# The last round in another order of units, with its first tiles' output and the feed-forward tiles in flight beside them

## The chip, the cores and the metric

The kernel runs on one core of one Trainium2 chip. The metric is device time in microseconds (us) of one execution, lower is better. The engines are TensorE (PE: matmuls into the PSUM banks; PEld: its weight loads), VectorE (DVE), ScalarE (ACT), GpSimd (POOL) and SyncE (SP, which issues DMAs). Each works through its own instructions in order and waits on semaphores for the others.

## The reference

One pre-norm transformer layer in float32 for 4 batches of 1024 tokens of width 128: attention with 16 heads of width 64, then a gated feed-forward layer of width 352 whose inputs and weights are rounded blockwise to FP4 values.

```python
def fp4_quant_dequant(x):                       # blocks of 16 along the last dim
    scale = jnp.maximum(jnp.max(jnp.abs(xb), axis=-1, keepdims=True) / 6.0, 1e-12)
    idx = jnp.searchsorted(_MID, jnp.abs(xb / scale))
    return (_GRID[idx] * jnp.sign(xb / scale) * scale).reshape(x.shape)
def fp4_linear(x, w):
    return jnp.einsum('bsk,nk->bsn', fp4_quant_dequant(x), fp4_quant_dequant(w))
# attention: e = exp(sim - max); attn = e / (sum(e) + 1e-10); out = (attn @ v) @ Wo.T + bo
x = x + attention(layernorm(x))
n = layernorm(x)
x = x + fp4_linear(silu(fp4_linear(n, w_gate)) * fp4_linear(n, w_up), w_down)
```

## The kernel before

**Rounds and units.** The 64 pairs of batch and head are taken two heads at a time: 32 pairs (NPAIR), one for each round. There are 34 rounds, 0 to 33; a round attends its own pair, projects keys, queries and values for the next one, and finishes the output of the one before. A round has four units k = 0 to 3, each one head with one half (512 rows) of the queries, and a unit has eight slots s = 0 to 7, one for each 128 keys. Unit k was head k // 2, half k % 2: both halves of head 0, then both of head 1. Round 33 has no units left; it holds the last unit's products with the values and what remains of pair 32.

**A slot.** TensorE makes two matmuls of scores into one of two banks (L628, L630), ScalarE takes the exponential (L781), GpSimd subtracts its rounded part (L475, "product" or "low part" in what follows), and TensorE multiplies the unit before with the values (L655, L657, L650). TensorE may run only two slots ahead of the exponentials. After each unit ScalarE copies the result (L750), VectorE makes the denominator and its reciprocal (L946, L948), and ScalarE scales (L791, in slots 3 and 4 of the unit behind the copy).

**Jobs.** All other matmuls are jobs in the table JOBS (L51): a name, a bank, and the places (unit, slot) at which TensorE, ScalarE and VectorE do their parts. `t` turns the normalised output, half 0 or 1; `o` projects it and VectorE adds it to x (L940). `x`, `g`, `u`, `h`, `d` are the feed-forward layer of two token tiles at a time: turn the input, gate, up, turn the hidden values, down. Between `u` and `h` the hidden values are quantised in ten steps (`quant`, L1088) at the places AT_H_BEGIN and AT_H (L66): nine on VectorE, and one, a scaling called the rounding step here, on ScalarE (`lift_steps`, L1139, at AT_H_LIFT). `runs` (L105) says in which rounds a job is done, `job_before`, `job_ready` and `job_ahead` (L124 to L148) which job's semaphore a wait names. Feed-forward tiles start as soon as their batch is through attention; the last two before the tail (n = 11) have `g` and `u` in round 32 and `h` and `d` in round 33.

**The tail.** The last batch's eight tiles can be normalised only when pair 32 is added. VectorE takes statistics of four tiles (`late_stats`, L1428), GpSimd the root (L1331), VectorE normalises and quantises them (`late_x`, L1440), for half 0 and then half 1. The last step of a quantisation is GpSimd's (`end`, L1320). Then come four groups of two tiles: TensorE gate and up (L1371, L1372), ScalarE the tanh, GpSimd the gate product (L1344), VectorE the product with up and the next quantisation (L1466, L1103 to L1125), TensorE the turn and down (L1379, L1386). In round 33, VectorE did the statistics of half 0 at (1, 7) and those of half 1 and `late_x(0)` at (2, 7):

```python
                            if (k, s) == (2, 7):
                                dve.wait_ge(s_x2, 2 * NPAIR)
                                ffn.late_stats(dve, x2, 1)

                                dve.wait_ge(s_pv, 4 * NPAIR)
                                ffn.late_x(dve, x2, 0)
```

Of the kernel before, what the change touches and what calls it, by code (L numbers as in the profile page):

```python
# [15 lines left out]
P = 128  # L16
# [43 lines left out]
        ("v1", X0, (3, 5), (3, 6), (3, 6))]  # L60
# [14 lines left out]
AT_X_LIFT, AT_H_LIFT = (3, 5), (0, 5)  # L75
FIRST_FFN = PAIRS + 1
# [46 lines left out]

def job_before(r, n):  # L124

    for back in range(2):
        if r - back < 0:
            return None
        for m in reversed(range(n if back == 0 else len(JOBS))):
            if JOBS[m][1] == JOBS[n][1] and runs(r - back, m):  # L130
                return m, back
    return None


def job_ready(g, r, n):

    def of(r, last=len(JOBS)):
        return sum(1 for m in range(last) if JOBS[m][1] == JOBS[n][1] and runs(r, m))
    return sum(of(a) for a in range(r)) + of(r) * (g - r) + of(r, n + 1)
# [33 lines left out]
def build(nc, x, wq, wk, wv, wo, bo, w_gate, w_up, w_down, out):  # L173
    with ExitStack() as ctx:
# [124 lines left out]
        def output_of(g, q, k):  # L299

            pq, pk = (q, k - 2) if k >= 2 else (1 - q, k + 2)
            return 4 * (g - 1) + k - 2, pq, pk // 2, (pk % 2) * IT

        def taken(m, g):
# [7 lines left out]
            if name[0] == "t":  # L312
                return s_ot, 2 * (g - 2) + c + 1
            if name[0] == "o":
                return s_x2, 2 * (g - 2) + c + 1
# [25 lines left out]
        def _(sp):  # L341
# [9 lines left out]
            def round_(g, r, q):  # L351
                prev, cur, nxt = flags(r)

                def place_max(k):

                    head, half = (k + 1) // 2 % 2, (k + 1) % 2
# [124 lines left out]
        def _(pe):  # L481
# [45 lines left out]
            def job(name, g, r, q, n):  # L527
# [27 lines left out]
                elif name[0] == "t":  # L555

                    wait(pe, s_on, 8 * (g - 1) - 2 * (1 - c))
                    for t in range(4):
                        last = pe.transpose(bank[:, t * P:(t + 1) * P], o_n[1 - q][:, 4 * c + t, :], ident[:, :])  # L559
                elif name[0] == "o":  # L560

                    wait(pe, s_ot, 2 * (g - 2) + c + 1)
                    for t in range(4):
                        last = pe.matmul(bank[:, t * P:(t + 1) * P], oT[:, (4 * c + t) * P:(4 * c + t + 1) * P],  # L564
                                         wo_s[:, bass.ds((g - 2) % PAIRS, 1), :].rearrange("p a n -> p (a n)"),
# [14 lines left out]
            def round_(g, r, q):  # L580
# [6 lines left out]
                for k in range(4):  # L587
                    head, half = k // 2, k % 2
                    unit = 4 * (g - 1) + k

                    def scores(d):

                        n = 2 * q + 1 if k < 2 else 2 * (1 - q)
                        h = n % 2
                        if k % 2 == 0 and d == 0:
                            wait(pe, s_dkh[h], 32 * (g + (1 if k else 0)))
                            wait(pe, s_dqh[h], 32 * (g + (1 if k else 0)))
# [904 lines left out]
```

## Time and profile before

| | us |
|---|---|
| median of 3 runs | 1441.13 (1439.35 to 1445.4) |
| the profiled execution, device time | 1440.82 |
| its span | 1437.8 |
| PE busy | 1341.8 (93%) |
| DVE busy | 1123.0 (78%) |
| ACT busy | 1134.4 (79%) |
| POOL busy | 1143.5 (80%) |
| exponentials, L781, 1024 of them | 775.3 |
| POOL products, L475, 1024 of them | 1080.3 |

Times in the profile count from the span's start. An instruction's row gives its start and length; "idle" is how long its engine stood before it, and the arrow names what released it. A busy share is an average over stages: the change touches only what lies between some 1352 us (unit 2 of round 32) and 1395 us, so those stages are what to read. The last unit's exponentials end at 1369.95, the last VectorE instruction begins at 1435.27.

### The profile page before, as it was taken

Reading aid. Unit: us, or ns where it says so; the run is one execution under the profiler, and the core shown is the slowest. Engines: PE = TensorE matmul, PEld = TensorE weight load, DVE = VectorE, ACT = ScalarE, POOL = GpSimd, SP = SyncE. Lnnn points to the kernel's source line nnn. Section 1 sums busy time; section 2 is a strip of 40 time slices with the busy share of each in tenths; the row PEclk is TensorE's granted clock in tenths of the full one; section 3 lists DMA queues with packets and bytes.
Section 4 is the critical chain, followed back from the end, with each engine's and each line's share of the span. In section 5 each row is a group of like instructions: output and inputs, shape, how many; then the busy total and the mean of one; then the engine's idle time right before and its main releaser. Section 6 shows DMA issues by size and latency. Waiting matters only on the chain.

```text
span 1437.8 us, 43018 instructions
## 1 busy us (share of the span) xinstructions
PE 1341.8 (93%) x17924; PEld 880.5 (61%) x17924; DVE 1123.0 (78%) x1717; ACT 1134.4 (79%) x2285; POOL 1143.5 (80%) x1135
## 2 busy tenths in 40 slices
PE   3899999999999999999999999999999999999956
PEld 2466666666666666666666666666666666666644
DVE  7777777778778878787887878888787888878677
ACT  2698887978888887888788888888888888788842
POOL 5688988878888878788887888888888888888832
PEclk8899999999999999999999999999999999999986
DMA  7111111112211111122111111211122121112000
GB/s 178 46 46 46 46 41 28 28 42 46 46 46 46 29 44 28 46 50 46 46 28 34 40 46 45 50 35 38 24 49 46 46 50 24 42 31 50 2 5 15
DMA packets 46687, 60.26 MB, mean 42 GB/s; under 512 B 8672, under 2 KB 21920, under 8 KB 46496
## 3 DMA queue, kind: packets, MB, share of 16 engines
q1 hardware_dynamic: 46336, 57.26, 17.0%
q8 instruction: 143, 2.34, 0.7%
q14 instruction: 48, 0.39, 0.1%
q10 hardware_dynamic: 160, 0.26, 0.1%
HBM read 4.80 MB, written 2.10 MB: 5 GB/s over the span
## 4 chain that ended last, share of the span: by engine, by line
PE 69%; DVE 21%; ACT 6%; issue 3%; DMA 1%; POOL 1%; SPq 0%; DVEq 0%
PE st L628 13%; PE st L630 11%; DVE negm L959 8%; PE sm L610 8%; PE ob L650 7%; PE ob L657 6%; PE ob L655 6%; ACT probs L781 3%; PE sm L548 2%; PE sm L1258 2%; PE mb L564 2%; PE sm L564 2%; DVE qv L1113 2%; PE mb L548 2%; PE sm L553 2%
## 5 line engine op out<-in xcount | busy, mean ns | idle before, releaser
L475 POOL TENSOR_TENSOR p_low<-probs 128x512 f16<-128x512 f32 x1024 | 1080.3, 1075 | 231.7 <-ACT probs L781 214.2
L781 ACT ACTIVATE probs<-st,lift,exp_scale 128x512 f32<-128x512 f32 x1024 | 775.3, 772 | 164.2 <-PE st L630 156.3
L959 DVE TENSOR_REDUCE negm<-sm 128x1 f32<-128x1024 f32 x512 | 616.2, 1214 | 204.8 <-PE sm L610 204.5
L628 PE MATMUL st<-q_hl,k_hh 128*128 128x512 f16 x1024 | 391.9, 383 | 6.8 <-ACT probs L781 6.7
L630 PE MATMUL st<-q_hm,k_l 128*128 128x512 f16 x1024 | 388.9, 380 | 0.0
L655 PEld LDWEIGHTS ob<-v,probs 128*128 128x128 bf16 x4096 | 289.7, 99 | 60.9 <-ACT o_raw L750 1.1
L655 PE MATMUL ob<-v,probs 128*128 128x65 f16 x4096 | 319.3, 193 | 0.7 <-ACT o_raw L750 0.7
L657 PE MATMUL ob<-v,probs 128*128 128x64 f16 x4096 | 319.8, 194 | 0.0
L657 PEld LDWEIGHTS ob<-v,probs 128*128 128x128 bf16 x4096 | 270.6, 97 | 59.9
L650 PEld LDWEIGHTS ob<-v,p_low 128*128 128x128 f16 x4096 | 177.1, 97 | 90.7 <-issue 1.1
L628 PEld LDWEIGHTS st<-q_hl,k_hh 128*128 128x128 f16 x1024 | 99.5, 97 | 154.3 <-issue 80.4
L650 PE MATMUL ob<-v,p_low 128*128 128x65 f16 x4096 | 188.1, 193 | 0.0
L610 PE MATMUL sm<-k_hh,q_hl 64*128 64x512 f16 x512 | 155.7, 384 | 10.7 <-DMA q_hm<-q_high 3.8
L610 PE MATMUL sm<-k_hh,q_hm 64*128 64x512 f16 x512 | 156.2, 385 | 0.0
L791 ACT ACTIVATE o_n<-o_raw,rden 128x64 f32<-128x64 f32 x512 | 147.1, 337 | 1.1 <-DVE rden L948 1.1
L630 PEld LDWEIGHTS st<-q_hm,k_l 128*128 128x128 f16 x1024 | 100.2, 98 | 26.8 <-issue 9.5
L716 ACT ACTIVATE oT<-sm 128x512 f32<-128x512 f32 x64 | 38.2, 597 | 37.4 <-PE sm L559 37.0
L946 DVE TENSOR_SCALAR den<-o_raw 128x4 f32<-128x4 f32 x128 | 51.4, 402 | 8.4 <-ACT o_raw L750 8.4
L564 PE MATMUL sm<-wo_s,oT 128*128 128x128 f32 x256 | 36.8, 287 | 20.7 <-DVE negm L959 19.3
L610 PEld LDWEIGHTS sm<-k_hh,q_hl 64*128 64x128 f16 x512 | 29.1, 94 | 34.5 <-issue 11.2
L750 ACT ACTIVATE o_raw<-ob 128x260 f32<-128x260 f32 x128 | 50.0, 390 | 0.0
L564 PEld LDWEIGHTS sm<-wo_s,oT 128*128 128x128 f32 x256 | 31.2, 192 | 22.5 <-DVE negm L959 20.9
(204 smaller groups left out, 1640.6 us busy)
## 6 DMA issues: line engine op xcount, KB each, us to landing
k_hh<-k_high SPq DMA_DIRECT2D x128, 128.0 KB, 2.4
k_l<-k_low SPq DMA_DIRECT2D x64, 128.0 KB, 2.4
q_hl<-q_high SPq DMA_DIRECT2D x64, 128.0 KB, 2.3
q_hl<-q_low SPq DMA_DIRECT2D x64, 128.0 KB, 2.4
q_hm<-q_high SPq DMA_DIRECT2D x62, 128.0 KB, 2.3
x<-x SPq DMA_DIRECT2D x4, 512.0 KB, 7.3
q_hm<-m_high SPq DMA_DIRECT2D x128, 1.0 KB
q_hm<-m_low SPq DMA_DIRECT2D x128, 1.0 KB
```

The costliest lines, as they stand in the source:

```text
L475: return pool.tensor_tensor(p_low[b][:, j, :], p, p.bitcast(BF16)[:, 1::2], ALU.subtract)
L548: last = pe.matmul(bank[:, :], of_pair(wT[w], "qk".index(name[0]), g), of_batch(xT[a], g, c * HALF, HALF), start=(w == 0 and a == 0), stop ...
L564: last = pe.matmul(bank[:, t * P:(t + 1) * P], oT[:, (4 * c + t) * P:(4 * c + t + 1) * P], wo_s[:, bass.ds((g - 2) % PAIRS, 1), :].rearran ...
L610: last = pe.matmul(sm_banks[2 * (1 - a) + h], q_rows[rows, t * P:(t + 1) * P], k_hh[n][rows, h * 512:(h + 1) * 512], start=True, stop=True)
L628: pe.matmul(st[s % 2][:, :], k_hh[n][:, s * P:(s + 1) * P], q_hl[n][:, half * HALF:(half + 1) * HALF], start=True, stop=False)
L630: pe.matmul(st[s % 2][:, :], k_l1[n][:, s * P:(s + 1) * P], q_hm[n][:, half * HALF:(half + 1) * HALF], start=False, stop=True).then_inc(s_ ...
L650: last = pe.matmul(ob[:, o:o + VC], p_low[1 - k % 2][:, j, t * P:(t + 1) * P], v_j[:, 1:1 + VC], start=False, stop=(j == JT - 1), skip_gro ...
L655: pe.matmul(ob[:, o:o + VC], p, v_j[:, 1:1 + VC], start=(t == 0 and j == 0), stop=False, skip_group_check=True)
L657: pe.matmul(ob[:, o + 1:o + VC], p, v_j[:, 1 + VC:1 + VC + DH], start=False, stop=False, skip_group_check=True)
L781: nc.scalar.activation(probs[k % 2][:, s, :], st[s % 2][:, :], ACT.Exp, bias=lift[:, 0:1], scale=exp_scale[:, head, pair:pair + 1]).then_i ...
L791: last = nc.scalar.activation(o_n[pq][:, tile + t, head * DH:(head + 1) * DH], o_raw[k % 2][:, t, 1:VC], ACT.Copy, scale=rden[:, k % 2, t: ...
L959: nc.vector.tensor_reduce(negm[k % 2][:, pair % 4:pair % 4 + 1], banks.rearrange("p a n -> p (a n)"), AX.X, ALU.max, negate=True).then_inc ...
```

## The change

In round 32 the units take half 0 of head 0, half 0 of head 1, then the two halves 1 (`head_half`). So half 0 of both heads is through after unit 1 instead of unit 2. That lets `t0` and `o0` of pair 32 stand in round 32 at unit 3, slots 5 and 6, and the statistics of half 0 at (3, 7); `late_x(0)` stands at (0, 0) of round 33, and GpSimd does the first quantisation's last step ahead of the second root. For the two tiles in flight `g1` and `u1` move from unit 3 (slots 1 and 2) to unit 2 (slots 5 and 6), their quantisation from round 33 to unit 3 of round 32 (AT_H_LAST), and `h0`, `h1`, `d` to slots 2, 3 and 5 of round 33's first unit, between the last unit's products. The jobs are the same in number and size. `job_before` and `job_ready` now sort by place instead of by position in the table. The gate product on VectorE also waits on `s_hm`, in all rounds.

```diff
-        ("v1", X0, (3, 5), (3, 6), (3, 6))]
+        ("v1", X0, (3, 5), (3, 6), (3, 6)),
+        ("g1", X0, (2, 5), (2, 6), (2, 6)), ("u1", X1, (2, 6), None, (2, 7)),
+        ("t0", X1, (3, 5), (3, 6), None), ("o0", X0, (3, 6), None, (3, 7)),
+        ("h0", MB, (0, 2), (0, 3), None), ("h1", X1, (0, 3), (0, 4), None), ("d", X0, (0, 5), None, (0, 6))]
+LAST = len(JOBS) - 7
+AT_H_LAST, AT_H_LAST_LIFT = ((3, 0), (3, 0), (3, 1), (3, 3), (3, 4), (3, 5)), (3, 2)
...
+def whose(r, n):
+    return r if n >= LAST else r - 1
...
+    if n >= LAST:
+        return r == (NPAIR + 1 if name in "hd" else NPAIR)
+    if (JOBS[n][0] in ("g1", "u1") and r == NPAIR) or (JOBS[n][0] in ("t0", "o0", "h0", "h1", "d") and r == NPAIR + 1):
+        return False
...
+def head_half(r, k):
+    return (k % 2, k // 2) if r == NPAIR else (k // 2, k % 2)
...
-                    head, half = k // 2, k % 2
+                    head, half = head_half(g, k)
...
+                        if r == NPAIR and (k, s) == (3, 7):
+                            dve.wait_ge(s_x2, 2 * NPAIR - 1)
+                            ffn.late_stats(dve, x2, 0)
                         if r == NPAIR + 1:
-                            if (k, s) == (1, 7):
-                                dve.wait_ge(s_x2, 2 * NPAIR - 1)
-                                ffn.late_stats(dve, x2, 0)
+                            if (k, s) == (0, 0):
+                                dve.wait_ge(s_pv, 4 * NPAIR - 1)
+                                ffn.late_x(dve, x2, 0)
                             if (k, s) == (2, 7):
                                 dve.wait_ge(s_x2, 2 * NPAIR)
                                 ffn.late_stats(dve, x2, 1)
-                                dve.wait_ge(s_pv, 4 * NPAIR)
-                                ffn.late_x(dve, x2, 0)
...
-        if n is not None and here == AT_H_LIFT:
+        if n is not None and r <= NPAIR and here == AT_H_LIFT:
+            self.lift_steps(act, 2 * FF, self.steps(n, True))
+        n = ffn_two(r, 1)
+        if n is not None and r == NPAIR and here == AT_H_LAST_LIFT:
             self.lift_steps(act, 2 * FF, self.steps(n, True))
...
-            for part, place in enumerate(AT_H_BEGIN):
+            for part, place in enumerate(AT_H_LAST if r == NPAIR else AT_H_BEGIN):
...
             dve.wait_ge(self.s_th, 2 * n + t + 1)
+            wait(dve, self.s_hm, 2 * n + t)
...
         root(0)
+        self.end(pool, 0)
         root(1)
-        self.end(pool, 0)
         self.end(pool, 1)
```

**VectorE around unit 3 of round 32.** `den` and `rden` are a unit's denominator and reciprocal, `wgu` and `hidden` the gate and up products of the tiles in flight, `q_small`, `qv`, `qw` the scratch of their quantisation. Before:

```order
L946 TENSOR_SCALAR den<-o_raw1 128x4 [waits o_taken]
L948 RECIPROCAL rden<-den 128x4 [waits sums_made]
L1289 SCALAR_TENSOR_TENSOR wgu<-xn,sm 128x352 [waits tanh_made,mb_ready1]
L1293 SCALAR_TENSOR_TENSOR hidden<-wgu,sm 128x352 [waits gate_taken,mb_ready2]
L1103 TENSOR_REDUCE q_small<-hidden 128x44 [waits hidden_made]
L1105 TENSOR_SCALAR q_small<-q_small 128x44 [waits quant_step]
L946 TENSOR_SCALAR den<-o_raw0 128x4 [waits o_taken]
L948 RECIPROCAL rden<-den 128x4 [waits sums_made]
L1109 TENSOR_SCALAR q_small<-q_small 128x44 [waits quant_step]
L1111 RECIPROCAL q_small<-q_small 128x44 [waits quant_step]
L1113 TENSOR_TENSOR qv<-hidden,q_small 128x704 [waits quant_step]
L1118 TENSOR_SCALAR qw<-qv 128x704 [waits quant_step]
```

And now:

```order
L1320 SCALAR_TENSOR_TENSOR wgu<-xn,sm 128x352 [waits hidden_made,tanh_made,mb_ready1]
L1324 SCALAR_TENSOR_TENSOR hidden<-wgu,sm 128x352 [waits gate_taken,mb_ready2]
L973 TENSOR_SCALAR den<-o_raw1 128x4 [waits o_taken]
L975 RECIPROCAL rden<-den 128x4 [waits sums_made]
L1130 TENSOR_REDUCE q_small<-hidden 128x44 [waits hidden_made]
L1132 TENSOR_SCALAR q_small<-q_small 128x44 [waits quant_step]
L1136 TENSOR_SCALAR q_small<-q_small 128x44 [waits quant_step]
L1138 RECIPROCAL q_small<-q_small 128x44 [waits quant_step]
L1140 TENSOR_TENSOR qv<-hidden,q_small 128x704 [waits quant_step]
L1145 TENSOR_SCALAR qw<-qv 128x704 [waits quant_step]
```

Gate and up stand ahead of unit 1's reciprocal instead of behind it, and the quantisation up to the mask (`qw<-qv`) follows it in one piece, where the reciprocals of units 2 and 3 stood around it.

**ScalarE at the start of unit 3 of round 32.** `o_raw1` is the copy of unit 1's result, `probs1` the exponentials, `xn<-sm` the tanh of g1, `qw<-qw` the rounding step. Before:

```order
L750 ACTIVATE o_raw1<-ob 128x260 [waits pv_done]
L781 ACTIVATE probs1<-st,lift,exp_scale 128x512 [waits pv_done,scores_t_ready]
L781 ACTIVATE probs1<-st,lift,exp_scale 128x512 [waits scores_t_ready]
L1278 ACTIVATE xn<-sm 128x352 [waits mb_ready1]
L781 ACTIVATE probs1<-st,lift,exp_scale 128x512 [waits scores_t_ready] x2
L791 ACTIVATE o_n1<-o_raw1,rden 128x64 [waits norm_step]
L791 ACTIVATE o_n1<-o_raw1,rden 128x64
```

And now:

```order
L776 ACTIVATE o_raw1<-ob 128x260 [waits pv_done]
L807 ACTIVATE probs1<-st,lift,exp_scale 128x512 [waits pv_done,scores_t_ready]
L807 ACTIVATE probs1<-st,lift,exp_scale 128x512 [waits scores_t_ready]
L1170 ACTIVATE qw<-qw 128x704 [waits quant_step]
L807 ACTIVATE probs1<-st,lift,exp_scale 128x512 [waits scores_t_ready] x2
```

The tanh left this place, and the rounding step stands here, behind two exponentials and ahead of six.

**VectorE in round 33.** `x2<-x2,sm 128x512` and `x2<-x2,mb 128x512` are the additions of o0 and o1, the one of 128x256 that of d, `p_low0<-x2` the normalisation of four tiles. Before, from the last unit's reciprocal to the first normalisation:

```order
L946 TENSOR_SCALAR den<-o_raw1 128x4 [waits o_taken]
L948 RECIPROCAL rden<-den 128x4 [waits sums_made]
...
L940 TENSOR_TENSOR x2<-x2,mb 128x512 [waits x2_added,mb_ready0]
L1297 TENSOR_TENSOR x2<-x2,sm 128x256 [waits mb_ready1]
L1433 BN_STATS stats<-x2 128x6 [waits x2_added]
...
L1445 TENSOR_SCALAR p_low0<-x2,mv,rstd 128x128 [waits ln2_root_step,pv_done]
L1445 TENSOR_SCALAR p_low0<-x2,mv,rstd 128x128 x3
L1103 TENSOR_REDUCE wd<-p_low0 128x32 [waits ln2_done]
```

And now, from the first normalisation through the last unit's reciprocal to the second statistics:

```order
L1476 TENSOR_SCALAR p_low0<-x2,mv,rstd 128x128 [waits ln2_root_step,pv_done]
L1476 TENSOR_SCALAR p_low0<-x2,mv,rstd 128x128 x3
...
L1152 TENSOR_TENSOR probs0<-probs0 128x512 [waits quant_step]
L1328 TENSOR_TENSOR x2<-x2,sm 128x256 [waits mb_ready1]
L973 TENSOR_SCALAR den<-o_raw1 128x4 [waits o_taken]
L975 RECIPROCAL rden<-den 128x4 [waits sums_made]
L967 TENSOR_TENSOR x2<-x2,mb 128x512 [waits x2_added,mb_ready0]
L1464 BN_STATS stats<-x2 128x6 [waits x2_added]
L1464 BN_STATS stats<-x2 128x6 x3
L1468 BN_AGGR mv<-stats 128x2 [waits ln2_stats_step]
```

The last unit's denominator and reciprocal stood ahead of both statistics and both normalisations; now they stand behind the first normalisation and its quantisation.

## Rows read from the trace of the kernel before

**Rows 1.** Busy time: length, then PE, PEld, DVE, ACT, POOL (with instructions), clock, DMA.

```profile
1361.60:1370.20 8.60, 7.73 (x115) 5.17 (x114) 3.36 (x6) 7.51 (x15) 8.29 (x9) 1.00 0.01 2
1370.20:1382.60 12.40, 8.78 (x138) 7.63 (x138) 9.95 (x29) 5.29 (x17) 2.60 (x4) 1.00 0.02 4
```

**Rows 2.** Chain of waits, 1388 to 1398 us; start, length, engine, tile, line.

```profile
1391.43 1.54 PE st L1371 x2
...
1397.25 0.94 POOL probs L1344
```

**Rows 3.** Timeline of ScalarE from unit 3 on; start, length, instruction, count, idle time before.

```profile
1361.42 0.38 ACT L750 ACTIVATE o_raw<-ob 128x260 f32<-128x260 f32 x1
1361.69 1.45 ACT L781 ACTIVATE probs<-st,lift,exp_scale 128x512 f32<-128x512 f32 x2
...
1363.82 0.78 ACT L781 ACTIVATE probs<-st,lift,exp_scale 128x512 f32<-128x512 f32 x1
...
1367.70 2.25 ACT L781 ACTIVATE probs<-st,lift,exp_scale 128x512 f32<-128x512 f32 x3
...
1373.61 0.79 ACT L1143 ACTIVATE qw<-qw 128x704 f32<-128x704 f32 x1 [1.69 <-DVE qw L1118]
```

**Rows 4.** Timeline of VectorE: reciprocal, six steps of the hidden quantisation, one without GpSimd.

```profile
1362.22 0.18 DVE L948 RECIPROCAL rden<-den 128x4 f32<-128x4 f32 x1
...
1365.53 0.89 DVE L1103 TENSOR_REDUCE q_small<-hidden 128x44 f32<-128x704 f32 x1
1366.45 0.90 DVE L1105 TENSOR_SCALAR q_small<-q_small 128x44 f32<-128x44 f32 x1
...
1371.66 0.43 DVE L1111 RECIPROCAL q_small<-q_small 128x44 f32<-128x44 f32 x1
1372.12 0.89 DVE L1113 TENSOR_TENSOR qv<-hidden,q_small 128x704 f32<-128x704 f32 x1
1373.05 0.53 DVE L1118 TENSOR_SCALAR qw<-qv 128x704 uint32<-128x704 uint32 x1
...
1399.69 0.18 DVE L1105 TENSOR_SCALAR wd<-wd 128x44 f32<-128x44 f32 x1
```

**Rows 5.** Timeline of VectorE from the last reciprocal to the second quantisation's end.

```profile
1375.44 0.18 DVE L948 RECIPROCAL rden<-den 128x4 f32<-128x4 f32 x1
...
1379.81 0.69 DVE L940 TENSOR_TENSOR x<-x,mb 128x512 f32<-128x512 f32 x1 [0.58 <-PE mb L564]
...
1382.68 1.08 DVE L1445 TENSOR_SCALAR p_low<-x,mv,rstd 128x128 f32<-128x128 f32 x4
...
1388.32 1.85 DVE L1445 TENSOR_SCALAR p_low<-x,mv,rstd 128x128 f32<-128x128 f32 x4
...
1394.12 0.69 DVE L1125 TENSOR_TENSOR probs<-probs 128x512 f32<-128x512 f32 x1
```

**Rows 6.** Timeline of TensorE: projection, turns, output projection, down projection, a slow turn.

```profile
1362.51 0.84 PE L1258 MATMUL sm<-wguT,xn 128*128 128x352 f32 x2
...
1376.86 0.63 PE L559 MATMUL sm<-ident,o_n 128*128 128x128 f32 x4 [0.42 <-ACT o_n L791]
...
1378.62 1.16 PE L564 MATMUL mb<-wo_s,oT 128*128 128x128 f32 x8
1379.61 1.50 PE L1269 MATMUL sm<-wdT,hiddenT 128*128 128x128 f32 x12
1389.63 1.11 PE L1362 MATMUL sm<-ident,p_low 128*128 128x128 f32 x4 [8.52 <-POOL p_low L1325]
```

**Rows 7.** Timeline of GpSimd: the last twelve products and the first root.

```profile
1358.98 12.61 POOL L475 TENSOR_TENSOR p_low<-probs 128x512 f16<-128x512 f32 x12 [0.86 <-ACT probs L781]
...
1379.60 1.01 POOL L1338 TENSOR_TENSOR rstd<-var_eps,minus_half 128x4 f32<-128x4 f32 x1
```

**Rows 8.** Stretches of one us on TensorE: length, busy time, granted clock, DMA.

```profile
1384.00:1385.00 1.00, 0.00 (x0) 1.00 0.00 0
1385.00:1386.00 1.00, 0.00 (x0) 0.50 0.00 0
```

More of the change, by code:

```diff
@@ L121, in runs, with jobs_of, job_ready @@
     return cur if JOBS[n][ON_PE][0] < 3 else nxt
+def jobs_of(r, bank):
+    return sorted((m for m in range(len(JOBS)) if JOBS[m][1] == bank and runs(r, m)), key=lambda m: (JOBS[m][ON_PE], m))
 def job_before(r, n):
[L126 to L139, printed above, removed]
+    here = jobs_of(r, JOBS[n][1])
+    at = here.index(n)
+    if at:
+        return here[at - 1], 0
+    earlier = jobs_of(r - 1, JOBS[n][1]) if r else []
+    return (earlier[-1], 1) if earlier else None
+def job_ready(r, n):
+    here = jobs_of(r, JOBS[n][1])
+    return sum(len(jobs_of(a, JOBS[n][1])) for a in range(r)) + here.index(n) + 1
+def head_half(r, k):
+    return (k % 2, k // 2) if r == NPAIR else (k // 2, k % 2)
 def has_max(r, k):
@@ L299, in output_of @@
         def output_of(g, q, k):
-            pq, pk = (q, k - 2) if k >= 2 else (1 - q, k + 2)
-            return 4 * (g - 1) + k - 2, pq, pk // 2, (pk % 2) * IT
+            pq, r, pk = (q, g, k - 2) if k >= 2 else (1 - q, g - 1, k + 2)
+            head, half = head_half(r, pk)
+            return 4 * (g - 1) + k - 2, pq, head, half * IT
         def taken(m, g):
@@ L555, in job @@
                 elif name[0] == "t":
-                    wait(pe, s_on, 8 * (g - 1) - 2 * (1 - c))
+                    pair, own = whose(g, n), whose(g, n) == g
+                    wait(pe, s_on, 8 * pair - (4 if pair == NPAIR else 2) * (1 - c))
                     for t in range(4):
-                        last = pe.transpose(bank[:, t * P:(t + 1) * P], o_n[1 - q][:, 4 * c + t, :], ident[:, :])
+                        last = pe.transpose(bank[:, t * P:(t + 1) * P], o_n[q if own else 1 - q][:, 4 * c + t, :], ident[:, :])
                 elif name[0] == "o":
-                    wait(pe, s_ot, 2 * (g - 2) + c + 1)
+                    pair = whose(g, n)
+                    wait(pe, s_ot, 2 * (pair - 1) + c + 1)
                     for t in range(4):
                         last = pe.matmul(bank[:, t * P:(t + 1) * P], oT[:, (4 * c + t) * P:(4 * c + t + 1) * P],
-                                         wo_s[:, bass.ds((g - 2) % PAIRS, 1), :].rearrange("p a n -> p (a n)"),
+                                         wo_s[:, bass.ds((pair - 1) % PAIRS, 1), :].rearrange("p a n -> p (a n)"),
                                          start=True, stop=True)
@@ L587, in round_ @@
                 for k in range(4):
-                    head, half = k // 2, k % 2
+                    head, half = head_half(g, k)
                     unit = 4 * (g - 1) + k
                     def scores(d):
[L593 to L597, printed above, removed]
+                        of = g if k < 2 else g + 1
+                        h, half = head_half(of, (k + 2) % 4)
+                        n = 2 * (q if k < 2 else 1 - q) + h
+                        if half == 0 and d == 0:
+                            wait(pe, s_dkh[h], 32 * of)
+                            wait(pe, s_dqh[h], 32 * of)
                         earlier = maxima_ahead(r, k, 4 * d - 1)
@@ L699, in take @@
                 cols = slice(c * HALF, (c + 1) * HALF)
-                ready = job_ready(g, r, m)
+                ready = job_ready(r, m)
                 if name[0] == "q":
@@ L1205, in beside_vector @@
         n = ffn_two(r, 2)
-        if n is not None:
+        if n is not None and r <= NPAIR:
             for part, place in enumerate(AT_H):
```

19 lines of the change are left out of this document (10 added, 9 removed).

## The prediction

> **What bounds the kernel now.** I read the stages first. In the last unit of the last round TensorE is busy 7.73 of 8.60 us, ScalarE 7.51 and GpSimd 8.29, while VectorE works only 3.36; in the stretch behind it VectorE works 9.95 of 12.40 [rows 1]. So the units are paced by three engines together, and behind them the end hangs on VectorE. Second, the chain of waits: the last step of the first quantisation is followed by gate and up on TensorE, a pair in 1.54 us, and later by GpSimd's second gate product, which begins at 1397.25 [rows 2]. Beside it runs the second quantisation, done at 1394.81 [rows 5]; everything later on VectorE is a fixed series behind these two. I call that time L. The question is what the change does to L, and whether what it gains before L is lost again earlier.
>
> **The two projections moved into unit 2 (g1, u1).** Each pair of matmuls stands with 0.84 us [rows 6]. They leave unit 3 and enter unit 2, so TensorE's sum over the two units doesn't change; but unit 2 ends later. Bounds 0 (all in waits) and 1.7 us (twice 0.84); I take 1.0, since some of it falls into waits that TensorE has there. The copy of unit 1's result, which opens unit 3 on ScalarE, moves from 1361.42 [rows 3] to 1362.4.
>
> **The quantisation moved into unit 3, and the wait that it brings.** Its rounding step on ScalarE (qw<-qw) stood in round 33, where nothing urgent was queued behind it. Now it stands third in unit 3, ahead of six exponentials. It waits for six VectorE instructions, which come behind the denominator and its reciprocal of unit 1; before, that reciprocal ended 0.98 us after the copy began (1361.42 to 1362.40) [rows 3, 4], so 1363.4 now. Then reduce 0.89, two steps on the block scales at 0.90 or 0.18, reciprocal 0.43, product 0.89, mask 0.53 [rows 4], and 0.15 of gaps: 4.7 us with the large figure twice, 3.25 with the small one. The large one was measured with GpSimd at work, the small one with GpSimd idle; GpSimd has its product of unit 3's second exponential until about 1365.7 and then nothing, so I take 4.1. The mask is ready at 1367.5 (1366.7 to 1368.1). With 0.79 for the rounding step [rows 3] the third exponential starts at E = 1368.3. Without the wait it could start when two exponentials behind the copy are done: 1362.4 + 0.27 + 1.45 = 1364.1. So ScalarE loses 4.2 us, 3.4 of it waiting, and all that is queued behind: six exponentials, and through them TensorE's scores and GpSimd's products.
>
> The Trainium skill (SBUF — State Buffer, section "SBUF: two separate sides") says that VectorE and GpSimd hold a shared port pair as an exclusive lock for a whole instruction. That speaks against this place, since it makes small VectorE steps wait out a GpSimd product; the trace agrees with its 0.90 beside 0.18. By the rule the wait would be at the long end while GpSimd runs and at the short end afterwards, which is the same middle.
>
> **t0 and o0 inside unit 3.** From the third exponential on, unit 3 took 1369.95 - 1363.82 = 6.1 us [rows 3]. Now ScalarE also copies the turned tile (0.6), TensorE turns it (0.63) and projects it (1.16) [rows 6], each waiting for the other. By steps: three exponentials and two pairs of scalings bring the sixth exponential to E + 3.0; the turn starts at E + 3.2 when the last scaling is done, the copy is ready at E + 4.5, the projection and the last scores are done at E + 6.1, the last exponential at E + 6.9. That is 0.8 more than before; bounds 0 and 2.4 (0.6 + 0.63 + 1.16 all exposed). Unit 3 ends at 1375.2 where it ended at 1369.95: **+5.2 us**, of which the wait is 3.4.
>
> **What is gained: the first half of the late tiles.** The sums for it now need only o0. Behind the last exponential GpSimd has one product (12.61 for twelve, so 1.05) and the root (1.01 [rows 7], some 1.35 with the small step ahead of it and the gaps): the root is ready at E + 9.4 = 1377.7. The first normalisation and quantisation therefore starts at 1377.7 instead of 1382.68, 5.0 us earlier though the unit ends 5.2 later. It takes 5.7 (from 1382.68 to the start of the next part at 1388.32 [rows 5]) and ends at 1383.4.
>
> **What that costs the second half.** The last unit's products start 0.3 behind its last exponential, 1375.5, take 3.0, now with two sets of transposes (0.4 each) and the down projection (1.35) between them, 5.1 in all; the copy of the result is done at 1380.9. Its reciprocal is queued on VectorE behind the first quantisation and the addition of d: 1383.4 + 0.4 + 0.4 = 1384.2. Before it was done at 1375.62 [rows 5]. From there the path is what it was: reciprocal to addition of o1 4.2 us (1375.62 to 1379.81), then 0.69 for the addition, 1.2 of statistics and 1.3 of root on an idle GpSimd, 5.7 of normalising and quantising (before 6.5, because its first part took 1.85 and not 1.08 [rows 5]). Sum: 1384.2 + 4.2 + 0.7 + 1.2 + 1.4 + 5.7 = 1397.4, so L moves by **+2.6**. Gate and up of the first tiles are then long done, so the second gate product follows the first directly, 0.4 less. And the turn and projection of the last output come after 4.5 us without matmuls: TensorE's last matmul ended at 1381.1 [rows 6], the granted clock was 1.00 (2.4 GHz) at 1384 and 0.50 (1.2 GHz) at 1385 [rows 8]; at half speed a turn of four tiles takes 1.11 and not 0.63 [rows 6], and the projection by the same ratio 2.0 and not 1.16, so +1.4 (bounds 0 and 1.4; I take 1.4, as a pause of 3.9 was enough there).
>
> The new wait of the gate product on hidden_made costs nothing: it stands between instructions of the same engine that are long done; bounds 0 and 24 times some 0.05, 1.2. The two swapped DMA destinations on SP are as long as before, and their data is ready a unit earlier than needed.
>
> **Sum.** +2.6 - 0.4 + 1.4 = +3.6. The profiled execution took 1440.82 for a span of 1437.8, 0.3 under the median of the runs, 1441.13. So 1444.4. What a measurement of this kernel can tell from no change is some 0.5%, 7.2 us.
>
> **Rivals.** (a) *The first half hides wholly.* The rounding step doesn't hold ScalarE, because unit 3 was slowed elsewhere anyway or VectorE's small steps run at 0.18: then the last exponential ends 3.4 earlier, and with the clock kept up L moves by +2.6 - 3.4 = -0.8, with the gate's -0.4 that is -1.2: 1439.6. For it: VectorE has 5.2 free us in unit 3 [rows 1]. Against: it is latency, not load, and the six instructions follow each other. A gain of 7 us isn't there: from the last reciprocal to L lie 13 us in series, and the last products can't end earlier than before.
>
> (b) *The wait cools TensorE.* During the 3.4 us in which ScalarE waits, TensorE runs out of work after its third group of products, since scores need free score banks. If the clock falls to 1.2 GHz there, the ten groups left in unit 3 run at half speed. TensorE's work in them is 4.6 us at full speed, about 3.2 of it would then be exposed: 1447.6, and up to 1450 if unit 3's last products are also slow. This is the case on the slower side; it decides from the point where the pause is as long as those before which the clock fell in this trace. For it: the wait is nearly as long as the pause of 3.9 us behind 1381.1, at whose end the clock fell [rows 6, 8]. Against: it held up to then, and my wait may be shorter still. The Trainium skill (TensorE: Matmul & The Clock Gate, Part 1) has the low clock as the resting state that activity lifts; by it this case would come to the same 1447.6.
>
> (c) *The order isn't what decides.* L stays with GpSimd and the gates, and both effects vanish: 1441.
>
> **Chances.** Forecast 0.50, (a) 0.20, (b) 0.22, (c) 0.08. The forecast's own range is 1442 to 1447; with (a) below and (b) above the range is 1437.5 to 1450. Faster by over 0.5% (below 1433.9) would need (a) and a luckier clock in the tail: 0.05. Slower by over 0.5% (above 1448.3): the far part of (b), 0.15. Within: 0.80.
>
> **What would show it.** In the changed profile ScalarE's qw<-qw in unit 3 should be preceded by 3 to 4 us of idle time released by VectorE's mask, GpSimd should idle as long, and the last exponential should end near 1375. VectorE's first late normalisation should start near 1378, the last output's reciprocal directly behind the addition of d, and VectorE should idle some 4 us before the addition of o1. I am wrong if the rounding step finds its input ready, if the last exponential ends before 1372, or if the second quantisation ends before 1394.

## The result and the profile after

The changed kernel took 1445.11 us (1443.44 to 1446.82, 20 runs), the kernel before 1439.88 us (1437.14 to 1445.4, 20 runs): ratio 1.0034, 95% interval 1.0027 to 1.0041, or 4.9 us (3.9 to 5.9) longer. It is a small loss.

The profiled execution after has a span of 1443.7 us against 1437.8. The two rows below, the copy on ScalarE that opens unit 2 of round 32, before (L750) and after (L776), show that it is 1.45 us later after, ahead of every instruction that the change moves. The shift was there early: ScalarE's copy of `m_high` begins at 33.12 before and 34.61 after. So the new wait of the gate product, which stands in all rounds, cost nothing that shows.

```profile
1352.21 0.40 ACT L750 ACTIVATE o_raw<-ob 128x260 f32<-128x260 f32 x1
```

```profile
1353.66 0.39 ACT L776 ACTIVATE o_raw<-ob 128x260 f32<-128x260 f32 x1
```

Over the profiles of all kernels below this offset lies between -0.02 and +2.03 us, the same kernel run twice differed by 0.75 and 1.56, and the time outside the span was 3.02 us before and 1.9 after, which nearly cancels it. So from here on times in a unit are counted from this copy, written +x. The last VectorE instruction starts at +83.06 before and +87.55 after: **4.5 us** later, which is what the two profiles give for the change.

ScalarE after, from the copy that opens unit 3 (columns as in [rows 3]):

```profile
1363.86 0.38 ACT L776 ACTIVATE o_raw<-ob 128x260 f32<-128x260 f32 x1
1364.12 1.45 ACT L807 ACTIVATE probs<-st,lift,exp_scale 128x512 f32<-128x512 f32 x2
1369.32 0.79 ACT L1170 ACTIVATE qw<-qw 128x704 f32<-128x704 f32 x1 [3.74 <-DVE qw L1145]
1370.01 1.43 ACT L807 ACTIVATE probs<-st,lift,exp_scale 128x512 f32<-128x512 f32 x2
...
1377.85 0.78 ACT L807 ACTIVATE probs<-st,lift,exp_scale 128x512 f32<-128x512 f32 x1 [1.25 <-PE st L656]
```

Unit 3 opens at +10.20 (before +9.21). The rounding step waits 3.74 us for VectorE's mask and holds six exponentials; the last of them ends at +24.97, where it ended at +17.74 [rows 3]. That last one also waited 1.25 for scores from TensorE; most of this wait isn't the clock's, since it is 1.07 in fill below, where the clock stays up: the projection of o0 stands ahead of those scores. TensorE's clock did fall in the pause. Its last matmul ahead of it began at 1366.79; length, busy time and granted clock of three stretches of one us:

```profile
1368.00:1369.00 1.00, 0.00 (x0) 1.00 0.00 0
1369.00:1370.00 1.00, 0.00 (x0) 0.83 0.00 0
1370.00:1371.00 1.00, 0.17 (x1) 0.50 0.00 0
```

The next matmul, at 1370.83, found 1.2 GHz, and so did the rest of unit 3 up to 1376. VectorE after, the steps in front of the wait (answering to [rows 4]) and the end of unit 3 into the second late normalisation ([rows 5]):

```profile
1365.23 0.85 DVE L1130 TENSOR_REDUCE q_small<-hidden 128x44 f32<-128x704 f32 x1
1366.12 1.00 DVE L1132 TENSOR_SCALAR q_small<-q_small 128x44 f32<-128x44 f32 x1
1367.15 0.18 DVE L1136 TENSOR_SCALAR q_small<-q_small 128x44 f32<-128x44 f32 x1
1367.37 0.43 DVE L1138 RECIPROCAL q_small<-q_small 128x44 f32<-128x44 f32 x1
1367.83 0.89 DVE L1140 TENSOR_TENSOR qv<-hidden,q_small 128x704 f32<-128x704 f32 x1
1368.76 0.53 DVE L1145 TENSOR_SCALAR qw<-qv 128x704 uint32<-128x704 uint32 x1
...
1381.10 1.11 DVE L1476 TENSOR_SCALAR p_low<-x,mv,rstd 128x128 f32<-128x128 f32 x4 [1.12 <-POOL rstd L1369]
...
1386.78 0.41 DVE L1328 TENSOR_TENSOR x<-x,sm 128x256 f32<-128x256 f32 x1
1387.11 0.91 DVE L973 TENSOR_SCALAR den<-o_raw 128x4 f32<-128x4 f32 x1
1388.05 0.18 DVE L975 RECIPROCAL rden<-den 128x4 f32<-128x4 f32 x1
1393.42 0.69 DVE L967 TENSOR_TENSOR x<-x,mb 128x512 f32<-128x512 f32 x1 [5.19 <-PE mb L589]
...
1396.84 1.11 DVE L1476 TENSOR_SCALAR p_low<-x,mv,rstd 128x128 f32<-128x128 f32 x4 [1.41 <-POOL rstd L1369]
```

The last unit's result was copied at 1384.25; its reciprocal came only behind the first quantisation and the addition of d. TensorE stood meanwhile, and its turn and projection ran at half clock:

```profile
1389.47 1.09 PE L583 MATMUL sm<-ident,o_n 128*128 128x128 f32 x4 [5.26 <-ACT o_n L817]
1391.34 2.05 PE L589 MATMUL mb<-wo_s,oT 128*128 128x128 f32 x8 [0.78 <-ACT oT L742]
```

They took 0.63 and 1.16 before [rows 6]. GpSimd's step that ends the second quantisation:

```profile
1402.67 1.06 POOL L1356 TENSOR_TENSOR p_low<-probs,wd 128x512 f32<-128x512 f32 x1 [5.87 <-DVE probs L1152]
```

That is +49.01, before +42.68: 6.3 us later. From there to the last VectorE instruction the program is the same, but it took 38.54 us in place of 40.38, so 1.8 us came back in the tail.

### The profile page after: what moved, and what is told of

It is laid out like the page before. It is cut to its first block, busy times and chain, and to the rows that moved or that the text cites. A ratio compares the mean times of both kernels' runs of the same rounds, so it can differ in the third digit from the quotient of the medians.

```text
span 1443.7 us, 43018 instructions
## 1 busy us (share of the span) xinstructions
PE 1349.1 (93%) x17924; PEld 884.4 (61%) x17924; DVE 1124.8 (78%) x1717; ACT 1134.5 (79%) x2285; POOL 1145.7 (79%) x1135
## 4 chain that ended last, share of the span: by engine, by line
PE 69%; DVE 21%; ACT 6%; issue 3%; POOL 1%; DMA 1%; SPq 0%; DVEq 0%
PE st L654 13%; PE st L656 11%; DVE negm L986 8%; PE sm L636 8%; PE ob L676 7%; PE ob L683 6%; PE ob L681 6%; ACT probs L807 3%; PE sm L571 2%; PE sm L1288 2%; PE mb L589 2%; PE sm L589 2%; DVE qv L1140 2%; PE mb L571 2%; PE sm L576 2%
## 5 line engine op out<-in xcount | busy, mean ns | idle before, releaser
L776 ACT ACTIVATE o_raw<-ob 128x260 f32<-128x260 f32 x128 | 50.0, 391 | 2.0 <-PE ob L676 1.8
L583 PE MATMUL sm<-ident,o_n 128*128 128x128 f32 x256 | 40.6, 282 | 5.7 <-ACT o_n L817 5.7
```

## The experiments

The theory ahead of the runs: the wait of ScalarE and the cold clock behind it cost some 5 us, the late last reciprocal some 3 more, and the unit order gains part of it back. The rivals are named in each expectation; where one speaks of GpSimd's first late product, it means `late_x(0)`, which runs on VectorE. The kernels with the last reciprocal ahead (rec_first, both, dve_both, order_only, spread and their repeats) have one edit more than their cuts below show: ahead of the tail's matmuls TensorE waits for the addition of d (`pe.wait_ge(ffn.s_fin, TWOS)`). In rec_first the tail's first turn still follows the matmul before it directly (1390.56), and in spread it waited 0.98 us for that addition. Three milestones of each profile, counted from the copy that opens unit 2: end of the last exponential; start of GpSimd's end of the second late quantisation; start of the last VectorE instruction. The last column is the distance from before that the ratio gives, with its interval.

| kernel | last exp. | second end | last DVE | runs: us against before |
|---|---|---|---|---|
| before | 17.74 | 42.68 | 83.06 | |
| changed | 24.97 | 49.01 | 87.55 | +4.9 (3.9 to 5.9) |
| lift_late | 23.29 | 47.46 | 87.61 | +3.9 (2.3 to 5.6) |
| fill | 23.34 | 47.50 | 87.29 | +4.2 (2.6 to 5.9) |
| rec_first | 24.83 | 45.81 | 84.26 | +1.3 (0.0 to 2.4) |
| both | 23.28 | 43.85 | 83.99 | +0.6 (-0.7 to 1.9) |
| flight_only | 23.35 | 47.83 | 87.91 | +6.0 (4.2 to 7.9) |
| dve_lift | 19.19 | 47.89 | 87.66 | +6.3 (4.3 to 8.2) |
| dve_both | 19.19 | 44.42 | 84.20 | +2.3 (1.0 to 3.5) |
| dve_thin | 19.20 | 43.14 | 83.29 | one run |
| order_only | 19.52 | 41.68 | 80.65 | -4.3 (-6.1 to -2.6) |
| order_again | 19.52 | 41.67 | 80.62 | -3.0 (-4.2 to -1.7) |
| spread | 19.51 | 38.62 | 77.61 | -4.0 (-5.5 to -2.4) |
| spread_again | 19.51 | 38.62 | 77.79 | -5.2 (-7.2 to -3.3) |

**lift_late: the rounding step three slots later.**

```diff
-AT_H_LAST, AT_H_LAST_LIFT = ((3, 0), (3, 0), (3, 1), (3, 3), (3, 4), (3, 5)), (3, 2)
+AT_H_LAST, AT_H_LAST_LIFT = ((3, 0), (3, 0), (3, 1), (3, 5), (3, 6), (3, 6)), (3, 5)
```

> Only the rounding step of the hidden quantisation and the three steps behind it stand later in unit 3 (slots 5 and 6 in place of 2 to 5). The wait theory: ScalarE's 3.74 us of idle time ahead of qw<-qw shrinks to under 0.7, TensorE has no long pause in unit 3 and keeps the full clock, so the last exponential ends 4 to 5.5 us earlier than in the changed kernel and the whole kernel is 3.5 to 6 us faster than it, 0 to 1.5 us slower than the kernel before. The rival, that the two added jobs t0 and o0 and not the wait make unit 3 long: less than 1 us of change against the changed kernel.

1444.53 us, ratio 1.0027 (1.0016 to 1.0039): about 1 us gained at most, not 3.5 to 6, and none at the last VectorE instruction (87.61 against 87.55). The wait was still 2.20 us, because VectorE's same six steps had grown. Its timeline:

```profile
1364.00 0.85 DVE L1130 TENSOR_REDUCE q_small<-hidden 128x44 f32<-128x704 f32 x1
1364.89 1.00 DVE L1132 TENSOR_SCALAR q_small<-q_small 128x44 f32<-128x44 f32 x1
1365.92 0.96 DVE L1136 TENSOR_SCALAR q_small<-q_small 128x44 f32<-128x44 f32 x1
1366.91 0.43 DVE L1138 RECIPROCAL q_small<-q_small 128x44 f32<-128x44 f32 x1
1367.38 1.21 DVE L1140 TENSOR_TENSOR qv<-hidden,q_small 128x704 f32<-128x704 f32 x1
1368.62 1.25 DVE L1145 TENSOR_SCALAR qw<-qv 128x704 uint32<-128x704 uint32 x1
```

The six take 5.70 us against 3.88 in the changed kernel, where GpSimd had run dry beside them. The ScalarE wait had starved GpSimd, and that had made VectorE fast: part of the cost hid the other part. Nor did TensorE keep the full clock. The copy of o0's turned tile now stood on ScalarE behind the waiting step, TensorE waited for it, and the projection ran at 0.50 of the clock; the last exponential then waited 2.41 us for its scores:

```profile
1371.99 2.05 PE L589 MATMUL sm<-wo_s,oT 128*128 128x128 f32 x8 [2.84 <-ACT oT L742]
```

**fill: fourteen extra score matmuls into a free bank while ScalarE waits** (their result is not used).

```diff
+                        if r == NPAIR and (k, s) == (3, 3):
+                            for _ in range(14):
+                                pe.matmul(sm_banks[0][:, :], k_hh[2 * q + head][:, 0:P],
+                                          q_hl[2 * q + head][:, 0:HALF], start=True, stop=True)
```

> The changed kernel with 14 extra matmuls of 512 columns (some 3 us at full clock) into a score bank that is free in that stage, behind TensorE's last work before its pause in unit 3; their result is read by nobody. ScalarE's wait stays at 3.7 us. If the clock is a cost of its own there: the granted clock stays at 1.00 through unit 3, the last exponential ends 1.5 to 2.5 us earlier than in the changed kernel, and the kernel is 1 to 2.5 us faster. If the slow clock is hidden behind ScalarE: no change within 0.5 us, or slower where the extra work delays the scores.

1444.66 us, ratio 1.0029 (1.0018 to 1.0041). This isolates the clock: the wait is untouched, the clock stays at 2.4 GHz through unit 3.

```profile
1368.24 0.79 ACT L1174 ACTIVATE qw<-qw 128x704 f32<-128x704 f32 x1 [3.74 <-DVE qw L1149]
...
1375.14 0.78 ACT L811 ACTIVATE probs<-st,lift,exp_scale 128x512 f32<-128x512 f32 x1 [1.07 <-PE st L656]
```

```profile
1363.00:1378.00 15.00, 12.81 (x185) 8.90 (x186) 11.51 (x22) 8.45 (x17) 11.14 (x11) 1.00 0.00 1
```

(Columns of the second as in [rows 1]; the clock is the 1.00 behind the counts.) The last exponential ends 1.63 us earlier. That is what the cold clock cost in unit 3. The end gains only 0.3 in the profile, since the tail took 39.79 us in place of 38.54; by the times it is 0.7, within the intervals.

**rec_first: the last unit's denominator and reciprocal inside the first late quantisation, behind its mask.**

```diff
-                        if s == 0 and (prev if k < 2 else cur):
+                        if s == 0 and (prev if k < 2 else cur) and (r, k) != (NPAIR + 1, 1):
...
-                                ffn.late_x(dve, x2, 0)
+                                ffn.late_x(dve, x2, 0, lambda: reciprocals(g, q, 1))
```

> Only the last unit's denominator and reciprocal on VectorE stand inside the first late quantisation (behind its mask) in place of behind it. If the queue behind that quantisation holds up the output projection o1: the reciprocal ends 2.5 to 3 us earlier, and o1's addition with it; TensorE's pause ahead of the last turn shrinks from 5.2 to some 2.4 us, so the clock may hold, 1.4 more. The kernel is 2.5 to 4.5 us faster than the changed one. Rival, that the second quantisation is held by something else (the root on GpSimd, or the first quantisation's own length): under 1 us.

1441.78 us, ratio 1.0009 (1.0000 to 1.0017): 3.6 us of the 4.9 gone, from one reciprocal's place. VectorE:

```profile
1385.30 0.16 DVE L974 TENSOR_SCALAR den<-o_raw 128x4 f32<-128x4 f32 x1
1385.50 0.18 DVE L976 RECIPROCAL rden<-den 128x4 f32<-128x4 f32 x1
...
1390.80 0.69 DVE L968 TENSOR_TENSOR x<-x,mb 128x512 f32<-128x512 f32 x1 [3.03 <-PE mb L589]
```

The last copy began at 1384.69 here and the reciprocal ended 0.99 us later; in the changed kernel it ended 3.98 us later. The second end comes 3.20 earlier. The part of the forecast on the clock didn't come: TensorE still stood 2.26 us ahead of the last turn, and turn and projection took 1.02 and 2.05.

**both: lift_late and rec_first together.**

> Both edits together. If the two costs are separate they add up: 6 to 10 us faster than the changed kernel, 2 to 5 us faster than the kernel before (ratio 0.9965 to 0.9985 to before). Rival, that one cost takes the other's place: no better than the better of the two alone.

1441.64 us, ratio 1.0004 (0.9995 to 1.0013). The gain is 4.3, not 6 to 10, as lift_late had already fallen short.

**flight_only: the tiles in flight as in the change; units, t0, o0 and the late tiles as before.**

```diff
-    return (k % 2, k // 2) if r == NPAIR else (k // 2, k % 2)
+    return k // 2, k % 2
...
-        ("t0", X1, (3, 5), (3, 6), None), ("o0", X0, (3, 6), None, (3, 7)),
```

> Only the in-flight tiles' part of the change: g1, u1, the last h tiles and d of the first half early, with the whole quantisation chain and its rounding step on ScalarE in unit 3 of the last round; units, score turns, late statistics and GpSimd's order as before. If the waiting rounding step is what costs (my theory: 3.7 us of ScalarE, a cold TensorE behind it, and about 1 us at unit 2), then this alone pays for it and gains only the gate: 3 to 5 us slower than before. The rival, that the costs come from the unit order and the late last reciprocal: within 1 us of before.

1444.52 us, ratio 1.0042 (1.0029 to 1.0055): this half of the change carries the whole loss, and somewhat more than the 3 to 5 us expected. Its rounding step waits the same 3.74 us for the mask.

**dve_lift: the rounding step on VectorE, so that ScalarE waits for nothing of the chain.**

```diff
+                    if part == 3:
+                        w = self.small[4][:, 0:2 * FF]
+                        dve.wait_ge(self.s_q, self.steps(n, True) + 6)
+                        nc.vector.tensor_scalar(w, w, MAGIC_HALF, None, ALU.mult).then_inc(self.s_q, 1)
```

> The changed kernel with the rounding step done on VectorE right behind the chain that makes it, so that ScalarE never waits for VectorE in unit 3 and the exponentials run through. Theory (the wait and the clock that fell in it are the cost): the last exponential ends 5 to 6 us earlier against the start of unit 3's copy, TensorE stays at the full clock through unit 3, and the kernel takes 4 to 6 us less than the changed one, so about 1440. Rival (VectorE's own queue sets the end, since GpSimd's products wait for the last reciprocal anyway): at most 2 us less.

1445.6 us, ratio 1.0044 (1.0030 to 1.0057). The local forecast held: last exponential 5.8 us earlier. The kernel gained nothing, which contradicts my theory and fits the number of its rival. Ten steps of the chain now stand on VectorE; some of them, the addition of o0 that follows, and GpSimd's products beside them:

```profile
1366.04 0.99 DVE L1132 TENSOR_SCALAR q_small<-q_small 128x44 f32<-128x44 f32 x1
...
1369.77 1.25 DVE L1145 TENSOR_SCALAR qw<-qv 128x704 uint32<-128x704 uint32 x1
1371.05 1.25 DVE L1234 TENSOR_SCALAR qw<-qw 128x704 f32<-128x704 f32 x1
1372.33 1.61 DVE L1155 SCALAR_TENSOR_TENSOR qv<-qw,qv 128x704 f32<-128x704 f32 x1
...
1375.62 0.89 DVE L1162 TENSOR_TENSOR hidden<-qv,q_small 128x704 f32<-128x704 f32 x1
1376.43 0.68 DVE L967 TENSOR_TENSOR x<-x,sm 128x512 f32<-128x512 f32 x1
```

```profile
1363.95 10.89 POOL L498 TENSOR_TENSOR p_low<-probs 128x512 f16<-128x512 f32 x9 [0.31 <-ACT probs L807]
```

From 1365.14 to 1376.51 the chain took 11.4 us and held the addition of o0, the statistics and the root behind it: the exponentials had finished at 1372.77, the reciprocal of unit 3 came at 1378.5. The queue had moved from ScalarE to VectorE. TensorE stood in it too, since the turn of the hidden values now stands between the last unit's products:

```profile
1376.66 0.87 PE L1295 MATMUL mb<-ident,hidden 128*128 128x128 f32 x3 [2.41 <-DVE hidden L1162]
```

So the second end came 1.1 us earlier (+47.89) for the 5.8 of the exponentials, and the tail took that back.

**dve_thin: dve_lift with GpSimd's eight products of unit 3 at 32 elements in place of 512** (the rest of the low part of that unit is left out).

```diff
-                            low_part(k % 2, s).then_inc(s_lp, 1)
+                            low_part(k % 2, s, 32 if (r, k) == (NPAIR, 3) else HALF).then_inc(s_lp, 1)
```

> dve_lift, in which GpSimd's eight products of unit 3 of the last round are 32 elements wide in place of 512 (the rest of that part of the output is left out). If VectorE's steps of the quantisation chain are long because GpSimd's products run beside them (theory), the nine steps behind the reciprocal take 7 to 8 us in place of the 11.2 of dve_lift, with the two-input steps at 0.9 us in place of 1.6. Rival (they are long from the queue of semaphores or from ScalarE and TensorE beside them): they stay within 10% of 11.2.

The same rows:

```profile
1364.65 0.19 DVE L1132 TENSOR_SCALAR q_small<-q_small 128x44 f32<-128x44 f32 x1
...
1366.48 0.53 DVE L1145 TENSOR_SCALAR qw<-qv 128x704 uint32<-128x704 uint32 x1
1367.04 0.53 DVE L1234 TENSOR_SCALAR qw<-qw 128x704 f32<-128x704 f32 x1
1367.60 0.89 DVE L1155 SCALAR_TENSOR_TENSOR qv<-qw,qv 128x704 f32<-128x704 f32 x1
...
1369.45 0.89 DVE L1162 TENSOR_TENSOR hidden<-qv,q_small 128x704 f32<-128x704 f32 x1
```

The ten steps (I had written nine) took 6.6 us in place of 11.4, even less than the 7 to 8 expected. One run took 1440.4 us; in its profile the last VectorE instruction starts 4.4 us earlier than in dve_lift. The second end came 4.75 us earlier, just what the chain had become shorter. So the chain is slow because GpSimd works beside it, and that is what swallowed dve_lift's gain. It also shows the end of this road, in one profile: without the wait and without that slowness the changed order only comes back to before (83.29 against 83.06), as the last reciprocal is still late.

**dve_both: dve_lift and rec_first.**

> The rounding step on VectorE as in dve_lift, and the last unit's reciprocal taken inside GpSimd's first late product, behind its mask and ahead of the rest of it. If the two costs are independent they add up: 7 to 9 us less than the changed kernel, 3 to 4 below before (1436 to 1438). If both act on the same chain (GpSimd's second product), the sum is no better than rec_first alone by more than 2 us: about 1440.

1441.45 us, ratio 1.0016 (1.0007 to 1.0024). The rival's number, not the sum. The three kernels with the reciprocal ahead stand at 84.26 (rec_first), 83.99 (both) and 84.20: the wait's removal brings nothing that shows beside it either, and the reciprocal's place brings its 3.5 us again (87.66 to 84.20).

**order_only: units, t0, o0 and the first half's statistics as in the change; the tiles in flight after the units as before; `late_x(0)` behind the last reciprocal.**

```diff
-        ("g1", X0, (2, 5), (2, 6), (2, 6)), ("u1", X1, (2, 6), None, (2, 7)),
...
-        ("h0", MB, (0, 2), (0, 3), None), ("h1", X1, (0, 3), (0, 4), None), ("d", X0, (0, 5), None, (0, 6))]
...
-                            if (k, s) == (0, 0):
+                            if (k, s) == (1, 4):
                                 dve.wait_ge(s_pv, 4 * NPAIR - 1)
                                 ffn.late_x(dve, x2, 0)
```

> Only the unit order of the last round, with the two score turns and the first half's late statistics early and the first late product between; the feed-forward tiles in flight stay where before has them, after the units. By the theory that the quantisation chain in unit 3 is the whole cost and the order the whole gain: 2 to 3 us faster than before, and spread (1435.1) is 1 to 2 us below it. Rival: the order gains nothing by itself, within 1 us of before.

1437.08 us, ratio 0.9970 (0.9958 to 0.9982): the other half of the change is a gain. In it the first late normalisation begins at +26.6, directly behind the chain's last step, and not at +30.5 as before:

```profile
1378.48 0.89 DVE L1161 TENSOR_TENSOR hidden<-qv,q_small 128x704 f32<-128x704 f32 x1
1379.29 1.11 DVE L1472 TENSOR_SCALAR p_low<-x,mv,rstd 128x128 f32<-128x128 f32 x4
```

**spread: order_only with the chain cut in two, its first six steps in unit 3, the rounding step behind unit 3's last exponential, the last reciprocal directly ahead of `late_x(0)`, and d's addition at (3, 0).**

```diff
+        ("d", X0, (2, 5), None, (3, 0))]
...
+AT_H_LAST = ((3, 3), (3, 4), (3, 5), (0, 0), (0, 0), (0, 0))
...
+        if n is not None and here == (AT_H_LIFT if r <= NPAIR else (0, 0)):
...
+            for part, place in enumerate(AT_H_LAST[:3] if r == NPAIR else AT_H_BEGIN):
+            for part, place in enumerate(AT_H if r <= NPAIR else AT_H_LAST[3:]):
```

> The unit order and early score turns of the change, the quantisation chain cut in two (its first half in unit 3 where ScalarE does not wait for it, the rounding step on ScalarE only after unit 3's last exponential), and the last reciprocal ahead of GpSimd's first product. Theory: nothing waits in unit 3, unit order gives GpSimd's products earlier: 4 to 5 us faster than before. Rival (order is not what decides, the tail takes back what is gained): within 1 us of before.

1435.08 us, ratio 0.9972 (0.9962 to 0.9983). Nothing in unit 3 waits for the chain any more; g1 and u1 are back in unit 3, and the last exponential ends at +19.51, as in order_only (+19.52), which has two of the six steps there:

```profile
1371.97 0.38 ACT L776 ACTIVATE o_raw<-ob 128x260 f32<-128x260 f32 x1
1372.24 0.79 ACT L1170 ACTIVATE qw<-qw 128x704 f32<-128x704 f32 x1
```

```profile
1376.18 0.18 DVE L975 RECIPROCAL rden<-den 128x4 f32<-128x4 f32 x1
1376.27 1.11 DVE L1473 TENSOR_SCALAR p_low<-x,mv,rstd 128x128 f32<-128x128 f32 x4
...
1385.34 1.11 DVE L1473 TENSOR_SCALAR p_low<-x,mv,rstd 128x128 f32<-128x128 f32 x4 [1.10 <-POOL rstd L1366]
```

The rounding step finds its input ready, the last reciprocal precedes the first late normalisation, and the second one starts at +32.8 where the changed kernel had it at +43.2.

**order_again and spread_again: the same two kernels on one chip**, since they had stood against different runs of before.

> The same kernel as order_only, on one chip with spread, since the two stood against different runs of before. In the profiles the last VectorE instruction came 80.65 us behind the copy that opens unit 2 here and 77.61 us in spread. If cutting the quantisation chain in two is worth what the profiles show, this kernel is 2 to 3 us slower than spread. If the tail takes that back, as the ratios 0.9970 and 0.9972 suggest, the two agree within 1 us.

> As spread: 2 to 3 us faster than order_again by the profiles, within 1 us of it by the ratios; 3 to 5 us faster than before in either case.

1438.49 and 1436.26 us, ratios 0.9979 (0.9971 to 0.9988) and 0.9964 (0.9950 to 0.9977): 2.2 us apart in the medians. The intervals of the two ratios still touch, but the runs can be compared directly: of the 55 pairs of a run of order_again (11) and one of spread_again (5), spread is the faster in 53, and the profiles say the same (2.8 to 3.0 us at the last VectorE instruction). So the cut of the chain gains some 2 us, and both kernels beat the one before.

## Why the prediction held, and where its sum was off

The forecast was 1444.4, the median 1445.11. That they lie 0.7 apart is partly luck: the forecast was 3.6 us above a profiled execution of 1440.82, and the kernel before had a median of 1439.88 in the comparison. The effect itself is +3.6 against +4.9 by the ratio and +4.5 by the profiles. Its terms by the profiles:

- **Unit 2 later by 1.0 for g1 and u1:** measured 0.99 (unit 3 opens at +10.20 in place of +9.21). Right, though it was a choice between 0 and 1.7; in order_only and spread, which leave them in unit 3, it opens at +9.20 and +9.19.
- **The wait in unit 3, 3.4 us:** measured 3.74. Right in kind, place and releaser. The six steps took 4.06 us with gaps, and I had taken 4.1; the reciprocal ahead of them ended 1.45 us behind the copy's start and not 0.98, since the denominator took 0.83 beside GpSimd's products.
- **t0 and o0 inside unit 3, 6.9 from the third exponential to the end of the last:** 6.98 in fill at the full clock (1368.94 to 1375.92). Right; at the half clock it took 8.62.
- **End of unit 3, +5.2:** measured +7.2. This is the step that was mis-sized: 1.6 by the clock and 0.3 by the later mask. I had put the clock's fall in the wait into a rival (b); it happened, so (b)'s mechanism was in the result too. But it cost 1.6 us there (fill) and not the 3.2 of the rival. TensorE was busy all of the six us from 1371 to 1377 here and 4.9 of the six from 1370 in fill, so part of its slow work filled time in which it would have stood.
- **From the last exponential to the copy of the last result, 5.7, with h0, h1 and d between the products:** measured 5.62. Right, and hidden, as VectorE came to that copy only 2.9 us later.
- **First late normalisation at the root of half 0:** I had it at 25.5 behind the copy; it came at +27.4, late by just what unit 3 was late.
- **The last reciprocal behind late_x(0):** right, and the dearest step of the order part. rec_first shows 3.2 us of it. The denominator in front took 0.91, not 0.2.
- **The cold turn and projection, +1.4:** measured 1.09 and 2.05 against 0.63 and 1.16, so 1.35. Right.
- **L, the end of the second quantisation, +2.6 and +1.4:** measured +6.3; 1.9 from unit 3, 0.7 from the denominator, less 0.4 between reciprocal and addition (5.19 against 4.2 + 1.4), and 0.1 over the rest.
- **The second gate, -0.4:** right (the first tail reduction starts 3.43 behind GpSimd's step in place of 3.88). What I had not seen is that the rest of the tail gave back 1.4 more: of the four groups' turns three took 1.07, 1.01 and 0.87 us at the clock that they happened to find, 1.49, 1.54 and 1.54 before. So two errors of opposite sign, +2.3 and -1.4, nearly met; that the total came this close is luck.

Rival (a) was wrong: the rounding step did hold ScalarE. But its price was wrong in a way worth keeping: dve_lift took the wait away and gained nothing. Rival (c), that the order decides nothing, is refuted by order_only and spread.

The books of the change, by the runs: the part on the tiles in flight costs 6.0 us (flight_only), the order with the reciprocal kept ahead gains 3.0 to 4.3 (order_only, twice), the reciprocal's new place costs 3.6 (rec_first). With the middle of the two that is 6.0 + 3.6 - 3.65 = 5.95, against 4.9 (3.9 to 5.9) measured; flight_only's own interval is 4.2 to 7.9.

What stays open: how the 6.0 us of flight_only split between the place of g1 and u1, the waiting step, the clock and the slow chain, since no run took them out of flight_only one by one, and why the tail meets another pattern of clock in each kernel. It took 38.45 to 40.38 us for the same instructions over these kernels (within 0.2 in the two pairs of repeats), and differences below some 2 us between two kernels can be that alone.

## What to carry to other kernels

When a step is moved into an earlier, full stage, ask first what is queued behind it on its engine, and place the waiting part of a chain only where nothing urgent follows: with the whole chain inside the unit and its matmuls moved along, the tiles in flight cost 6.0 us (flight_only), and six of its ten steps there cost the unit nothing when the rounding step stood behind the last exponential (spread). A tiny instruction that opens a long path (a reciprocal for a whole output) goes ahead of any long block on its engine. Removing a wait pays only as far as the next queue: look at what the freed engine will now run beside.

## What the runs showed of the hardware

How much a neighbour costs VectorE. Beside GpSimd's products of 128x512 the small step on 128x44 took 0.96 to 1.00 us and 0.18 to 0.19 without them; the mask on 128x704 1.25 and 0.53; the steps with two inputs 1.61 and 0.89; the reduction 0.85 and the reciprocal 0.43 either way (dve_lift and dve_thin). GpSimd paid as well: of nine products in 10.89 us in dve_lift, five took 1.04 each and the four beside the larger steps 1.31 to 1.69. The same six instructions sum to 3.88 us after, 5.70 in lift_late: in a trace with a stall in it, a neighbour's short durations may be the stall's own effect. The Trainium skill (SBUF — State Buffer, section "SBUF: two separate sides") has the port pair of the two engines locked for whole instructions, by VectorE steps with two inputs and by those in a two-port mode; the trace agrees in that steps with two inputs and the scalings grow while reduction and reciprocal don't, and in the waiting: in lift_late the two small steps end at 1365.89 and 1366.88, 0.05 and 0.04 us behind the ends of the products that began at 1364.80 and 1365.80 and took 1.04 each. In which mode a step ran, the trace doesn't show.

TensorE's clock fell in the pause of unit 3 while the engine stood: after the change it was 1.00 until 1369, 2.0 us behind the last matmul's end, 0.83 in the next us, and came back to 1.00 in 1377 with the engine busy since 1370.83. Keeping it busy with unneeded matmuls held the clock (fill), and was worth 1.6 us in the unit and 0.3 at the end.
